# Zero rows written by ScalarE, four slots for the first token exponentials, and another order of SyncE's transfers in an attention and soft-mixture block

## The chip, the core and the metric

The kernel runs on one core of a Trainium2 chip. The metric is the device time of one execution in microseconds. Three runs of the kernel before took 2685.64, 2686.21 and 2699.97 us, median 2686.21 us. TensorE multiplies matrices, VectorE reduces and combines, ScalarE evaluates functions and copies, GpSimd does side work, and SyncE only waits on semaphores and issues transfers. Each engine runs its own list of instructions in order; semaphores tie the lists together.

## The reference

The input x is 4 sequences of 2048 tokens with 256 features. The output is the sum of x and two branches of its layer norm:

```
x  = L0_attn_x;  xn = layernorm(x)
q, k, v = xn @ wq.T, xn @ wk.T, xn @ wv.T        # 16 heads of 16, 4 groups of keys and values
att = softmax(causal(q k / 4));  attention = (att v) @ wo.T
y  = layernorm(xn) * g + b;  se = layernorm(slot_embeds) * slot_g + slot_b
logits[n, e, s] = y[n] . se[e, s]                # 2048 tokens by 16*64 = 1024 slots, per sequence
dispatch = softmax(logits over the tokens); combine = softmax(logits over the 1024 slots)
slots = dispatch.T @ y;  eout[e] = (gelu(slots Wg + bg) * (slots Wu + bu)) Wd + bd
out = x + attention + combine @ eout
```

## The kernel before

There are five parts, one after the other: `project` (the projections), `attend`, `dispatch`, `experts`, `combine`. `attend` and `dispatch` share one block, so that an engine goes from the one into the other without a barrier. The diff touches the start of `attend` and the first half of `dispatch`.

**attend.** The 16 pairs of a sequence and a group of keys ("bg") each take 40 steps; a step s is one block of 128 keys against one chunk of 512 queries, for 4 heads. TensorE fills a ring of 7 PSUM banks with row-maximum products ("x", read by VectorE) and with score products ("s", read by ScalarE's exponentials, line 857, which write `pr`, a buffer of 4 steps by 4 heads by 512). The "x" work runs 22 steps ahead (`LEAD`), so the first 22 steps (-22 to -1, the lead) hold only "x" and, in steps -17 to -2, the early logits "l": 16 half tiles of the first 8 token tiles of `dispatch`. ScalarE copies each out of the ring (L844) into `pr`, which is still free, four half tiles to a buffer, and issues its transfer to DRAM (L847). At step 0 ScalarE waits until all 16 have landed, as the exponentials then write `pr`.

Queries and keys stand in groups of 64 rows of which the upper 32 are mostly zero. For group 0 GpSimd writes the zeros in `project`; for groups 1 to 3 SyncE issues 12 transfers (L737) from a zero tile, at the start of `attend`. Then its loop issues the row maxima (L749, as each comes out of VectorE), the loads of groups 1, 2 and 3 at steps -6, 6 and 46 (L533 to L542), and the context stores (L755).

**dispatch.** Phases: L0, L1, P(0,0), P(0,1), L2, P(1,0), P(1,1), L3, P(2,0), P(2,1), P(3,0), P(3,1). In a phase L of a sequence b, TensorE makes the logits of 16 token tiles (8 in L0), 12 matmuls each (L1364), into two pairs of PSUM banks. ScalarE copies each to SBUF (L1224); VectorE takes the row maximum (L1282) and the running column maximum (L1290). ScalarE then makes the token exponentials (L1197) of 1024 slots, n counting the 64 tiles, into `e1`, and SyncE stores each to DRAM (L1123). `e1` has 2 slots, so exponential n waits until store n-2 has landed. L0 and L1 hold 32 exponentials for 24 tiles. In the last 6 tiles of L1, L2, L3, VectorE also subtracts the column maximum from a half tile of the sequence before (L1253), and ScalarE exponentiates it (`exp_tile`, L1169), behind its copy and token exponential.

In a phase P(b, half) TensorE multiplies 16 tiles of these exponentials with rows y (L1381). The rows come in pairs of tiles m: SyncE loads a pair (L1093) into one of 4 places as soon as the multiplication has released it (`d_free`), and ScalarE scales it (L1179). In P(b,0) the first six tiles were exponentiated ahead; ScalarE's list there starts with the scaling of the fifth pair and only then has the exponential of tile 6. SyncE's list for a phase L has, at every fourth tile (t % 4 == 2), the load of the next 512 columns of y transposed (L1083), which waits until TensorE has finished tile t+1; in the last two tiles the loads of the fifth and sixth pair of y rows for the coming P phase; and the stores of exponentials.

## Time and profile before

| quantity | value |
|---|---|
| median of three runs | 2686.21 us (2685.64 to 2699.97) |
| the profiled execution | 2682.58 us, its span 2680.9 us |
| TensorE, VectorE, ScalarE, GpSimd busy | 2562.2, 2037.7, 1696.6, 432.2 us |
| start of `attend` to step 0 | about 154 to 213 us |
| phases L0 and L1 | 1767.2 to 1863.3 us |
| phases P(0,0) to L2 to P(1,0) | from 1852.9, 1.8 us per tile in P |
| L3 and what follows in `dispatch` | to about 2197 us |

### The profile page before, as it was taken

The numbers are of one execution on the slowest core, as the hardware profiler recorded it, in microseconds if no ns is written. First come the engines' busy times: TensorE is split into PE (matmuls) and PEld (weight loads), VectorE is DVE, ScalarE is ACT, GpSimd is POOL, SyncE is SP. The second block draws the span as 40 slices with busy tenths as digits, with TensorE's granted clock in tenths as the row PEclk, the third lists the DMA queues.
The fourth block names the chain that finished last, engine by engine and source line by source line (L and its number), as shares of the span: only waits on it lengthen the run. The fifth ranks groups of instructions, "written<-read, shape, count | busy, mean of one in ns | idle before, by whom it ended". The sixth has DMA issues, their size and how long they took to land. (4 is left out here: it accounts for less than half of the span.)

```text
span 2680.9 us, 47835 instructions
## 1 busy us (share of the span) xinstructions
PE 2562.2 (96%) x16291; PEld 1526.7 (57%) x16291; DVE 2037.7 (76%) x4879; ACT 1696.6 (63%) x3506; POOL 432.2 (16%) x677
## 2 busy tenths in 40 slices
PE   7988999999999999999999999988989999999999
PEld 4553444444444444444444444356877888889999
DVE  8877989989988989999999998946465523356665
ACT  5526777777777778777777777876656652122221
POOL 6711111111111111111111111323020100100000
PEclk9988999999999999999999999999999999999999
DMA  8995243303303303312321001045333364445554
GB/s 267 321 227 79 37 52 45 44 7 45 45 6 45 45 12 41 45 22 30 45 33 18 8 8 70 30 157 181 122 134 144 104 200 142 156 163 192 192 191 149
DMA packets 184110, 258.21 MB, mean 96 GB/s; under 512 B 57780, under 2 KB 134200, under 8 KB 182360
## 3 DMA queue, kind: packets, MB, share of 16 engines
q1 hardware_dynamic: 166040, 236.64, 35.0%
q10 hardware_dynamic: 17856, 18.88, 2.4%
q8 instruction: 114, 1.87, 0.3%
q14 instruction: 100, 0.82, 0.1%
HBM read 160.40 MB, written 89.16 MB: 93 GB/s over the span
## 5 line engine op out<-in xcount | busy, mean ns | idle before, releaser
L857 ACT ACTIVATE att_pr<-att_ring 128x512 f32<-128x512 f32 (+3 forms) x2560 | 1174.2, 548 | 333.1 <-PE att_ring L956 314.5
L923 DVE TENSOR_REDUCE att_mx<-att_ring 128x1 f32<-128x512 f32 x1536 | 967.9, 680 | 85.9 <-PE att_ring L969 83.5
L969 PE MATMUL att_ring<-att_ks,w_queries 48*128 48x512 f32 (+3 forms) x1920 | 647.0, 422 | 18.4 <-ACT att_pr L857 8.5
L956 PE MATMUL att_ring<-w_queries,att_ks 64*128 64x512 f32 (+3 forms) x1920 | 575.8, 406 | 6.3 <-DVE att_mx L929 2.3
L956 PEld LDWEIGHTS att_ring<-w_queries,att_ks 64*128 64x128 f32 x1920 | 300.7, 186 | 403.1 <-DVE att_mx L923 145.1
L929 DVE CUSTOM_DVE_ANT_0 att_junk<-att_ring,w_causal 128x256 bf16<-128x256 f32 (+3 forms) x1024 | 466.1, 486 | 60.4 <-PE att_ring L969 34.2
L1009 PE MATMUL att_acc<-att_pr,att_v 128*17 128x512 f32 (+3 forms) x3840 | 453.6, 544 | 2.7 <-ACT att_cT L868 1.5
L969 PEld LDWEIGHTS att_ring<-att_ks,w_queries 48*128 48x128 f32 x1920 | 307.0, 185 | 143.8 <-ACT att_pr L857 104.7
L803 POOL TENSOR_SCALAR_AFFINE_SELECT att_pr<-att_pr 128x512 f32<-128x512 f32 x256 | 163.0, 637 | 1042.5 <-ACT att_pr L857 1042.5
L969 PE MATMUL att_ring<-g_ks,w_queries 48*128 48x512 f32 (+3 forms) x640 | 208.3, 435 | 22.6 <-ACT att_pr L857 12.9
L1631 ACT CAST com_e1h<-com_tp 128x1024 fp32r<-128x1024 f32 x64 | 64.7, 1016 | 238.1 <-PE com_tp L1691 238.1
L956 PE MATMUL att_ring<-w_queries,g_ks 64*128 64x512 f32 (+3 forms) x640 | 197.3, 409 | 2.1 <-DVE att_mx L929 0.8
L1707 PE MATMUL com_mp<-pre_parts,com_e1h 128*128 x1024 | 186.7, 283 | 3.7 <-DVE com_e1l L1656 3.7
L956 PEld LDWEIGHTS att_ring<-w_queries,g_ks 64*128 64x128 f32 x640 | 103.3, 188 | 135.3 <-DVE att_mx L923 49.3
L1707 PEld LDWEIGHTS com_mp<-pre_parts,com_e1h 128*128 128x128 f32 x1024 | 158.9, 191 | 4.3 <-issue 4.3
L1009 PE MATMUL att_acc<-att_pr,g_v 128*17 128x512 f32 (+3 forms) x1280 | 152.0, 547 | 0.0
L1707 PE MATMUL com_mp<-pre_parts,com_e1l 128*128 x512 | 144.7, 283 | 0.0
L1009 PEld LDWEIGHTS att_acc<-att_pr,att_v 128*17 128x17 f32 x3840 | 78.0, 117 | 112.9 <-ACT att_pr L857 72.3
L969 PEld LDWEIGHTS att_ring<-g_ks,w_queries 48*128 48x128 f32 x640 | 99.4, 192 | 67.1 <-ACT att_pr L857 39.4
L1364 PE MATMUL dis_ps<-w_seTh,w_yTh 128*128 128x512 f32 x224 | 93.5, 417 | 24.7 <-ACT dis_lg L1224 14.8
L1381 PE MATMUL dis_ps<-dis_y,pre_parts 128*128 128x257 f32 x512 | 112.6, 380 | 4.2 <-ACT pre_parts L1169 4.2
L1381 PE MATMUL dis_ps<-dis_y,dis_lg 128*128 128x257 f32 x512 | 112.3, 380 | 1.8 <-ACT dis_lg L1169 1.8
(181 smaller groups left out, 3243.0 us busy)
## 6 DMA issues: line engine op xcount, KB each, us to landing
slot_exps<-dis_e SPq DMA_DIRECT2D x64, 512.0 KB, 2.8
com_e<-slot_exps SPq DMA_DIRECT2D x64, 512.0 KB, 3.6
w_queries<-q_parts SPq DMA_DIRECT2D x96, 256.0 KB, 12.0
q_parts<-w_queries SPq DMA_DIRECT2D x32, 512.0 KB, 5.0
dis_y<-in_L_attn_x_dram SPq DMA_DIRECT2D x64, 256.0 KB, 2.8
att_ks<-k_parts SPq DMA_DIRECT2D x72, 128.0 KB, 12.8
y_cols<-proj_yT SPq DMA_DIRECT2D x16, 512.0 KB, 5.3
w_yTl<-y_cols SPq DMA_DIRECT2D x16, 512.0 KB, 4.2
```

The costliest lines, as they stand in the source:

```text
L803: nc.gpsimd.affine_select(out=blk, in_=blk, compare_op=ALU.is_ge, fill=0.0, base=0, pattern=[[0, GS], [1, P]], channel_multiplier=-1).then ...
L857: nc.scalar.activation(pr[:, s % NPR, h, off:CH], spot(("s", s, h)), ACT.Exp, scale=float(HD) ** -0.5).then_inc(exp_done, 1)
L923: nc.vector.tensor_reduce(dst, spot(e), AX.X, ALU.max).then_inc(mb_used, 1)
L929: nc.vector.tensor_tensor_reduce(junk[:, h % 2, 0:wd], spot(e), w["causal"][:, CH - wd:CH], 1.0, LOW, ALU.add, ALU.max, dst).then_inc(mb_u ...
L956: nc.tensor.matmul(spot(e), ks[g][r, kb * P:(kb + 1) * P], qs[g][r, c, hf * CH + off:(hf + 1) * CH], start=True, stop=True).then_inc(sT_re ...
L969: nc.tensor.matmul(spot(e), qs[g][r, c, q0:q0 + P], ks[g][r, j * CH:j * CH + wd], start=True, stop=True).then_inc(mb_ready, 1)
L1009: last = nc.tensor.matmul(acc[VW * h:VW * h + HD + 1, off:CH], v[bg % NKV][:, kb // TPC, :, kb % TPC], pr[:, n % NPR, h, off:CH], start=(n ...
L1364: last = nc.tensor.matmul(ps[:, i % 2, 2 * (t % 2) + h, :], lhs[:, n % RING, k, (t % TPC) * P:(t % TPC + 1) * P], w[rhs][:, k, h * 512:(h ...
L1381: last = nc.tensor.matmul(ps[:, i % 2, q, 0:D + 1], lgs[b % 2][:, t, (hf * HB + q) * P:(hf * HB + q + 1) * P], y[:, m % NY, t % 2, 0:D + 1 ...
L1631: nc.scalar.copy(e1h[:, q].rearrange("p s n -> p (s n)"), tp[:, q, 0:2, :].rearrange("p a n -> p (a n)")).then_inc(e1h_kept, 1)
L1707: last = nc.tensor.matmul(mp[:, q, 0:D], lhs[:, q, s, :], rhs[:, b, s, :], start=(s == 0 and rhs is eoh and lhs is e1h), stop=(s == SB - 1 ...
```

## The change

1. SyncE's 12 zero transfers and the zero tile go. ScalarE writes the zeros by copies of a zero column, 32 partitions by 2048 elements each, 18 in all: 6 (group 1) before its first step, and one behind each of the first 12 early-logit copies (groups 2 and 3).
2. The last four early-logit transfers count on a semaphore of their own: step 0 waits for the first 12, step 3 for the last four.
3. The loads of groups 1 and 2 move from steps -6 and 6 to -2 and 10; the rows of ones of groups 1 to 3 count on the semaphore of the loads.
4. `e1` gets 4 slots for exponentials 0 to 31 (2 afterwards, when slots 2 and 3 hold the slot vectors, `sl` and `slT`); exponential 2 waits also for all context stores.
5. In `dispatch` SyncE issues a phase's stores of exponentials ahead of the load of y transposed, which moves from t % 4 == 2 to t % 4 == 3, and the fifth and sixth pair of y rows come behind all stores of the phase.

```diff
-    FIRST_LOADS = {-6: 1, 6: 2, 46: 3}
+    FIRST_LOADS = {-2: 1, 10: 2, 46: 3}
+    L_LATE = NL - GS
+    ZP = (QW + S) // S
...
-            for g in range(1, NKV):
-                for rg in range(NRG):
-                    r = slice(RG * rg + 32, RG * (rg + 1))
-                    for dst, n in ((queries[r, g * QW:(g + 1) * QW], QW), (ks[g][r, :], S)):
-                        sp.dma_start(dst.bitcast(F32).rearrange("p (k n) -> p k n", n=D),
-                                     w["zero"][r, :].bitcast(F32).unsqueeze(1)
-                                     .to_broadcast([32, n // D, D])).then_inc(zeroed[g], 16)
...
+            def zero_rows(k):
+
+                g, rg, n = 1 + k // (NRG * ZP), k // ZP % NRG, k % ZP
+                r = slice(RG * rg + 32, RG * (rg + 1))
+                rows = ks[g][r, :] if n == ZP - 1 else queries[r, g * QW + n * S:g * QW + (n + 1) * S]
+                nc.scalar.copy(rows, w["causal"][r, 0:1].to_broadcast([32, S])).then_inc(zeroed[g], 1)
+
+            for k in range(NRG * ZP):
+                zero_rows(k)
...
                         nc.scalar.copy(half_tile(e[1]), spot(e)).then_inc(l_kept, 1)
+                        if e[1] < (NKV - 2) * NRG * ZP:
+                            zero_rows(NRG * ZP + e[1])
...
-                                      half_tile(e[1])).then_inc(l_out, 16)
+                                      half_tile(e[1])).then_inc(l_out if e[1] < L_LATE else l_late, 16)
                 if s == 0:
-                    act.wait_ge(l_out, 16 * NL)
+                    act.wait_ge(l_out, 16 * L_LATE)
+                if s == NPR - 1:
+                    act.wait_ge(l_late, 16 * (NL - L_LATE))
...
-        e1 = a.sb("e1", [P, 2, NS])
+        e1 = a.sb("e1", [P, 4, NS])
...
+        WIDE = 2 * TPB
+        place = lambda n: n % 4 if n < WIDE else n % 2
+        stores_before = lambda n: n // 4 if n < WIDE else (WIDE // 4) + (n - WIDE) // 2
...
-                        if t % TPC == TPC - 2:
+                        store_exps(exps_by(b, t) if b < 2 else b * TPB + t + 1)
+                        if t % TPC == TPC - 1:
                             load_yT(b * CPB + t // TPC + RING)
-                        if b and t >= TPB - FIRST_Y:
-                            load_y(2 * (b - 1) * PAIRS + t - (TPB - FIRST_Y) + NY)
-                        store_exps(exps_by(b, t) if b < 2 else b * TPB + t + 1)
...
                     if b:
                         store_exps(b * TPB + TPB)
+                        for n in range(FIRST_Y):
+                            load_y(2 * (b - 1) * PAIRS + n + NY)
...
+                n = b * TPB + t
+                if n == 2:
+                    context_stored(act)
+                if stores_before(n):
+                    act.wait_ge(e_out[place(n)], 16 * stores_before(n))
```

ScalarE at the start of `attend`, kernel before (`att_pr` takes the early-logit half tiles):

```order
L844 COPY att_pr<-att_ring 128x512
L847 DMA first_logits<-att_pr 128x512
L844 COPY att_pr<-att_ring 128x512
L847 DMA first_logits<-att_pr 128x512
L844 COPY att_pr<-att_ring 128x512
```

and after, at the same place (`w_queries` and `att_ks` get their zero rows):

```order
L839 CAST w_queries<-w_causal 32x2048 x2
L839 CAST att_ks<-w_causal 32x2048
L839 CAST w_queries<-w_causal 32x2048 x2
L839 CAST att_ks<-w_causal 32x2048
L847 COPY att_pr<-att_ring 128x512
L839 CAST w_queries<-w_causal 32x2048
L852 DMA first_logits<-att_pr 128x512
L847 COPY att_pr<-att_ring 128x512
L839 CAST w_queries<-w_causal 32x2048
L852 DMA first_logits<-att_pr 128x512
```

Six pieces stand ahead of the first copy now, and one piece between each copy and its transfer.

SyncE from the last stores of L1 into P(0,0), before (`slot_exps` are the exponentials' stores, `dis_y` the pairs of y rows, `w_yTl` y transposed):

```order
L1123 DMA slot_exps<-dis_e 128x1024 x5
L1083 DMA w_yTl<-y_cols 128x1024
L1093 DMA dis_y<-in_L_attn_x_dram 128x2x256
L1123 DMA slot_exps<-dis_e 128x1024
L1093 DMA dis_y<-in_L_attn_x_dram 128x2x256
L1123 DMA slot_exps<-dis_e 128x1024 x2
L1125 DMA slot_sums<-dis_zr 128x16
L1093 DMA dis_y<-in_L_attn_x_dram 128x2x256 x10
```

and after:

```order
L1135 DMA slot_exps<-dis_e 128x1024 x4
L1095 DMA w_yTl<-y_cols 128x1024
L1135 DMA slot_exps<-dis_e 128x1024
L1137 DMA slot_sums<-dis_zr 128x16
L1105 DMA dis_y<-in_L_attn_x_dram 128x2x256 x12
```

The two pairs of y rows that were issued among the last stores now stand behind the last store and the sums. At the end of L2 one more thing stands ahead of them:

```order
L1135 DMA slot_exps<-dis_e 128x1024 x4
L1137 DMA slot_sums<-dis_zr 128x16
L1095 DMA w_yTl<-y_cols 128x1024
L1105 DMA dis_y<-in_L_attn_x_dram 128x2x256 x12
L1112 DMA slots<-dis_e 128x256 x4
```

There the load of y transposed comes between the last store and the y rows.

## Rows read from the trace of the kernel before

**Rows 1.** The page, part 1: busy us (share) and instructions.
```profile
PE 2562.2 (96%) x16291; PEld 1526.7 (57%) x16291; DVE 2037.7 (76%) x4879; ACT 1696.6 (63%) x3506; POOL 432.2 (16%) x677
```
**Rows 2.** Busy time by stretch, with granted clock, DMA share and GB/s.
```profile
160.00:204.00 44.00, 43.42 (x175) 25.39 (x174) 42.07 (x119) 9.39 (x16) 5.93 (x11) 0.92 0.99 211
213.80:225.40 11.60, 11.60 (x58) 5.38 (x58) 9.63 (x23) 7.47 (x19) 2.97 (x6) 0.50 0.00 0
...
1825.00:1830.00 5.00, 0.38 (x1) 0.39 (x2) 0.41 (x1) 5.00 (x10) 1.74 (x1) 0.63 0.26 105
```
**Rows 3.** ScalarE's timeline from the early logits to step 3.
```profile
166.47 0.59 ACT L844 COPY att_pr<-att_ring 128x512 f32<-128x512 f32 x1 [17.01 <-PE att_ring L980]
...
192.38 0.33 ACTq L847 DMA_DIRECT2D first_logits<-att_pr  x1
...
200.55 0.59 ACT L844 COPY att_pr<-att_ring 128x512 f32<-128x512 f32 x1 [1.67 <-PE att_ring L980]
...
213.11 2.23 ACT L857 ACTIVATE att_pr<-att_ring 128x512 f32<-128x512 f32 x5 [11.97 <-DMA first_logits<-att_pr]
...
220.36 0.38 ACT L857 ACTIVATE att_pr<-att_ring 128x256 f32<-128x256 f32 x1 [1.88 <-PE att_ring L956]
```
**Rows 4.** The early-logit transfer of 192.38 alone: issue to landing.
```profile
DMA to landing us min/median/max: 14.7/14.7/14.7
```
**Rows 5.** SyncE's timeline: the first transfer of the load of group 1.
```profile
188.05 0.40 SPq L533 DMA_DIRECT2D w_queries<-q_parts  x1
```
**Rows 6.** The form next to a zero piece: the page, part 5.
```profile
L1631 ACT CAST com_e1h<-com_tp 128x1024 fp32r<-128x1024 f32 x64 | 64.7, 1016 | 238.1 <-PE com_tp L1691 238.1
```
**Rows 7.** Waits of ScalarE, then of TensorE, from 1735 to 1850: total, times, longest.
```profile
ACT dis_e L1197 <- DMA slot_exps<-dis_e: 16.2, 9, 3.0
...
PE dis_ps L1364 <- ACT dis_lg L1224: 11.0, 6, 6.0
```
**Rows 8.** TensorE's timeline in L0 and L1.
```profile
1767.55 0.39 PE L1364 MATMUL dis_ps<-w_seTl,w_yTh 128*128 128x512 f32 x1
1767.78 0.40 PE L1364 MATMUL dis_ps<-w_seTh,w_yTl 128*128 128x512 f32 x1
...
1829.62 0.80 PE L1364 MATMUL dis_ps<-w_seTh,w_yTh 128*128 128x512 f32 x1 [5.95 <-ACT dis_lg L1224]
```
**Rows 9.** ScalarE's timeline from L0 to the start of P(0,0).
```profile
1770.31 1.02 ACT L1224 COPY pre_parts<-dis_ps 128x1024 f32<-128x1024 f32 x1 [3.15 <-PE dis_ps L1364]
1771.22 1.16 ACT L1197 ACTIVATE dis_e<-pre_parts,w_nr 128x1024 f32<-128x1024 f32 x1
...
1824.64 4.03 ACT L1179 ACTIVATE dis_y<-dis_y,w_yb,w_ys 128x256 f32<-128x256 f32 x8
...
1834.30 1.01 ACT L1224 COPY dis_lg<-dis_ps 128x1024 f32<-128x1024 f32 x1 [1.55 <-PE dis_ps L1364]
...
1848.82 0.99 ACT L1224 COPY dis_lg<-dis_ps 128x1024 f32<-128x1024 f32 x1
...
1853.37 0.99 ACT L1224 COPY dis_lg<-dis_ps 128x1024 f32<-128x1024 f32 x1
...
1864.45 1.08 ACT L1179 ACTIVATE dis_y<-dis_y,w_yb,w_ys 128x256 f32<-128x256 f32 x2
```
**Rows 10.** TensorE's timeline, tiles 6 to 13 of P(1,0).
```profile
1981.24 14.11 PE L1381 MATMUL dis_ps<-dis_y,dis_lg 128*128 128x257 f32 x64 [0.80 <-ACT dis_lg L1169]
```
**Rows 11.** SyncE's timeline at the end of L1 and of L2.
```profile
1864.95 0.43 SPq L1125 DMA_DIRECT2D slot_sums<-dis_zr  x1
...
1979.87 0.43 SPq L1125 DMA_DIRECT2D slot_sums<-dis_zr  x1
```
**Rows 12.** The load of y rows issued at 1980.47 alone: issue to landing.
```profile
DMA to landing us min/median/max: 3.2/3.2/3.2
```
**Rows 13.** VectorE's subtraction L1253 in L2, beside GpSimd's work and without it.
```profile
1955.79 2.83 DVE L1253 TENSOR_TENSOR dis_lg<-dis_lg,w_cm 128x512 f32<-128x512 f32 x1
...
1962.49 0.68 DVE L1253 TENSOR_TENSOR dis_lg<-dis_lg,w_cm 128x512 f32<-128x512 f32 x1
```

More of the change, by code:

```diff
@@ L347, in _ @@
                 nc.gpsimd.memset(w["ones"][:].bitcast(F32), 1.0).then_inc(zeroed, 1)
-                nc.gpsimd.memset(w["zero"][:].bitcast(F32), 0.0).then_inc(zeroed, 1)
-                pool.wait_ge(zeroed, 5)
+                pool.wait_ge(zeroed, 4)
                 tri = w["causal"][:, CH - P:CH]
@@ L681, in attend @@
         c_out = [sem(f"c_out{c}") for c in range(CPB)]
-        ones_set = [g0["ones_set"]] + [sem(f"ones_set{g}") for g in range(1, NKV)]
+        ones_set = g0["ones_set"]
+        ONES = lambda g: 16 * 2 * NRG if g else 0
         nm_max, cols_high, cols_split = sem("nm_max"), sem("cols_high"), sem("cols_split")
         acc_zeroed, v_ones = sem("acc_zeroed"), sem("v_ones")
-        l_split, l_kept, l_out, l_in = (sem(n) for n in ("l_split", "l_kept", "l_out", "l_in"))
+        l_split, l_kept, l_out, l_late, l_in = (sem(n) for n in ("l_split", "l_kept", "l_out", "l_late", "l_in"))
         nr, cm, nr_ready, cm_done = (first_logits[n] for n in ("nr", "cm", "nr_ready", "cm_done"))
@@ L722, in load @@
             def load(b, g):
-                for _ in load_group(sp, scr, b, g, qs[g], ks[g], v[g], loaded[g], zeroed[g] and (zeroed[g], 16 * 2 * NRG)):
+                for _ in load_group(sp, scr, b, g, qs[g], ks[g], v[g], loaded[g], zeroed[g] and (zeroed[g], NRG * ZP)):
                     pass
@@ L727, in load_first @@
                 load(0, g)
-                for _ in load_ones(sp, w, ks[g], ones_set[g]):
+                for _ in load_ones(sp, w, ks[g], loaded[g]):
                     pass
@@ L950, in _ @@
                         if h == 0 and n % NU in first:
-                            if bg < NKV and c == 0:
-                                pe.wait_ge(ones_set[g], 16 * 2 * NRG)
+                            if bg == 0 and c == 0:
+                                pe.wait_ge(ones_set, 16 * 2 * NRG)
                             pe.wait_ge(m_rows[c], 16 * NRG * (bg + 1))
@@ L1046, in dispatch @@
         y = a.sb("y", [P, NY, 2, D + 2])
[L1047 to L1049 removed]
         zr = a.sb("zr", [P, 2, TPB])
         rz = a.sb("rz", [P, SB])
[L1052 to L1053 removed]
+        lgs = [pre["lg"], a.sb("lg", [P, TPB, NS])]
+        e1 = a.sb("e1", [P, 4, NS])
+        nr, cm, nr_ready, cm_done = (first_logits[n] for n in ("nr", "cm", "nr_ready", "cm_done"))
+        sl = e1[:, 2].rearrange("p (q d) -> p q d", q=HB)
+        slT = e1[:, 3].rearrange("p (q e k j) -> p q e k j", q=HB, e=2, k=DK)
         ps = a.ps("ps", [P, 2, 4, 512])
@@ L1057, in dispatch @@
         y_in = [sem(f"y_in{q}") for q in range(NY)]
-        e_out = [sem(f"e_out{q}") for q in range(2)]
+        e_out = [sem(f"e_out{q}") for q in range(4)]
         z_out = [sem(f"z_out{q}") for q in range(2)]
@@ L1122, in store_exps @@
                     sp.wait_ge(e1_ready, n + 1)
-                    sp.dma_start(scr["e1"][b, t], e1[:, t % 2]).then_inc(e_out[t % 2], 16)
+                    sp.dma_start(scr["e1"][b, t], e1[:, place(n)]).then_inc(e_out[place(n)], 16)
                     if t == TPB - 1:
@@ L1156, in _ @@
             context_stored(sp)
+            for q in range(4):
+                sp.wait_ge(e_out[q], 16 * (stores_before(B * TPB) if q < 2 else WIDE // 4))
             for q in range(2):
-                sp.wait_ge(e_out[q], 16 * B * TPB // 2)
                 sp.wait_ge(z_out[q], 16 * B // 2)
@@ L1773, in block_kernel @@
             queries = b.sb("queries", [P, NKV * QW], F32R)[:]
-            w["causal"], w["zero"] = b.sb("causal", [P, CH]), b.sb("zero", [P, D], F32R)
+            w["causal"] = b.sb("causal", [P, CH])
             w["wqT"], w["wkvT"] = b.sb("wqT", [P, DK, D]), b.sb("wkvT", [P, DK, P])
```

29 lines of the change are left out of this document (13 added, 16 removed).

## The prediction

> **What bounds the kernel now.** I read the page first: TensorE is busy for 96% of the span, VectorE 76%, ScalarE 63% [rows 1]. So a change can win only where TensorE stands still or runs at its lower clock, or where it is made to. The stretches around the edits show two such places. The first is step 0 of `attend`: from 160 to 204 TensorE and VectorE are busy nearly throughout (43.4 and 42.1 of 44 us), and from 213.8 to 225.4 TensorE is fully busy but at a granted clock of 0.50, 1.2 GHz [rows 2]. Between them ScalarE waits 11.97 us, from 201.1 to 213.11, for the early-logit transfers to land [rows 3]; the ring is full of scores it should have read, and TensorE idles about 9.7 us. The second is L0 and L1: ScalarE waits 16.2 us in 9 waits for stores of exponentials, and TensorE waits for its copies, 11.0 us in the group that shows the most, the longest 6.0 [rows 7]. In the P phases TensorE runs without a gap: 64 matmuls, 8 tiles, in 14.11 us, 1.76 us a tile [rows 10]. Whatever delays it there is lost for good.
>
> **Edit 1, the zero rows.** SyncE's 12 transfers go. They were over before 188, when the load of group 1 starts [rows 5], and no wait in that stretch is on them, since TensorE and VectorE are the full engines there. Their going is worth nothing. ScalarE gets 18 pieces of 2048 elements. The trace has no such copy. From the 512-wide copy (0.59) [rows 3] and the 1024-wide cast (1.016) [rows 6] the slope is 0.426 us per 512, so 2048 take 1.016 + 2 x 0.426 = 1.87 us, the low bound; twice the 1.16 us of the 1024-wide exponential that reads SBUF [rows 9] is 2.32, the high one. I take 1.87, being nearest in kind. The Trainium skill, "ScalarE: Activation LUTs", section "Table sets: the hidden batching unit", gives 186 ns plus 0.833 ns per element for an instruction with immediate scale and bias, 1.89 us for 2048 elements as an estimate, and no run here shows it yet; by it the sum would be the same.
>
> The first six take 11.2 us from the start of `attend` at about 154.4 and end at 165.7, before the first copy at 166.47, ahead of which ScalarE idles 17.01 us: hidden. The next 12 stand between copies that come every (200.55 - 166.47)/15 = 2.27 us [rows 3]. Copy and piece take 0.59 + 1.87 = 2.46, so ScalarE falls behind 0.19 us each, 2.3 in all. TensorE needs a bank again seven fills later, a bit more than a step, so a copy may be late by about 2.27 - 0.59 = 1.7 us. Cost on the path: 0.6, taken 0.5. At 2.32 a piece it is 12 x 0.64 - 1.7 = 6.0 us.
>
> **Edits 2 and 3, the wait at step 0.** The twelfth transfer was issued at 192.38 and landed 14.7 us later, at 207.1 [rows 3, 4]. It is slow because the load of group 1 runs from 188.05 [rows 5], and that stays: in SyncE's list nothing waits between the row maxima of step -8 and step -2, so the new number moves no transfer. With the copies late by a little I take 207.6. Step 0 starts there instead of at 213.11: -5.5 us. The last four land by 213.1; step 3 first needs their places at 220.36 - 5.5 = 214.9 [rows 3], so their wait costs nothing, with 1.8 us to spare. TensorE's idle falls from 9.7 to some 4 us, and the slow stretch of 11.6 us behind it shrinks. At full clock VectorE's 9.63 busy us would set its length [rows 2], so at most 2.0 us are to be had; I take 1.0. Start of `attend` in all: -5.5 - 1.0 + 0.5 = -6.0, bounds -8.5 and +0.5. The later load of group 2 and the ones have some 50 steps of slack and cost nothing.
>
> **Edit 4, four slots.** Matmuls of a logit tile follow each other at 0.233 us, 12 to a tile: 2.80 us [rows 8]. From the copy of the first tile of L0 (1770.31) to that of the eleventh of L1 (1834.30) are 18 tiles and 64.0 us [rows 9]; TensorE's own pace is 18 x 2.80 = 50.4. ScalarE's work there is 18 copies at 0.91 (1770.31 to 1771.22), 26 exponentials at about 1.15 and 4.03 of y rows [rows 9]: 16.4 + 29.9 + 4.0 = 50.3 us. They fit, if it never waits for a store, and four slots give a store over three exponentials' time and the copies between, some 5 us. The y rows come in one piece at tile 7 of L1: 0.9 + 2.3 + 4.0 = 7.2 against two tiles of room, 5.6, so 1.6 late. That leaves 64.0 - 50.4 - 1.6 = 12.0 us; a half-speed stretch after this stop takes 0.5 back. Gain 11.5, bounds 13.6 (nothing late) and 4 (only the longest wait goes, part of it). The six last tiles of L1 don't get faster: there copy, maximum, column maximum, subtraction and `exp_tile` form one chain between ScalarE and VectorE of 1853.37 - 1848.82 = 4.55 us a tile, whatever the stores do. The new wait of exponential 2 for the context stores ends near 1771, and it comes after 1773: nothing.
>
> **Edit 5, the order of SyncE's transfers.** The stores no longer stand behind a wait for TensorE; that is in the 11.5. But the fifth and sixth pair of y rows, issued before the last store until now, come behind it and the sums. In L1 the sums are issued at 1864.95 and take 0.43 [rows 11], so the pair goes out at 1865.4 and lands 3.2 later [rows 12], at 1868.6. ScalarE scales it at 1864.45 today [rows 9], as the first thing in P(0,0), and tile 6's exponential is behind it. So TensorE, through with tile 5, stands 4.1 us longer. In L3 the same, 4.1. In L2 the load of y transposed, 512 KB, goes out between: the sums at 1979.87 + 0.43, then some 1.1 more than in L1, 5.2 us; TensorE starts tile 6 at 1981.24 after 0.80 idle [rows 10]. Together 13.4 us, on the path, since TensorE never catches up in P. Each idle of near 5 us will also lower the clock: after the 5.95 us before 1829.62 [rows 8] the stretch 1825 to 1830 had a granted 0.63 [rows 2] and the matmuls behind it were slow. I take 1.5 us each, 4.5 (between 0 and 2.5 each). Cost 17.9, bounds 10 (landing at 2.5, no clock loss) and 22.
>
> The load of y transposed comes up to a tile later; the columns have 8 tiles of slack. It also moves GpSimd's splitting. In L2 the subtraction takes 2.83 us beside GpSimd's and 0.68 without [rows 13], in the ScalarE-VectorE chain. Two of the meetings in L1 and L2 fall behind the phase now: -1, bounds -3 and +2. The Trainium skill, "GPSIMD Engine Reference", section "Specifications", says that GpSimd shares its SBUF interfaces with VectorE, with contention for VectorE instructions of two SBUF inputs; the subtraction is one, and the trace agrees (2.83 against 0.68). By that rule only where the meetings fall matters, and each may cost as much as this one.
>
> **Sum.** -6.0 - 11.5 + 17.9 - 1.0 = -0.6 us on the profiled execution's 2682.58 (span 2680.9), that is 2682.0. That execution stands 3.6 below the median of 2686.21, so 2685.6 in terms of the runs.
>
> **Rivals.** *Faster: the y rows are not on the path.* If ScalarE's list hid the late pair, or the data came before its turn, -18.5 would be left: 2668. For it: SyncE has little else to do there. Against it: ScalarE has the scaling ahead of tile 6's exponential, and TensorE waits 0.80 us at just this place already [rows 10].
> *Slower: late y rows at full price.* Place: tile 6 of P(0,0), P(1,0), P(2,0). Each stop costs 5 us and more of landing and 2.5 of clock, 22 in all, while the gain of L0 and L1 is 9: -5 - 9 + 22 = +8, 2694. It decides as soon as the three stops together exceed the two gains, 17 to 18 us. For it: after 5.95 us idle the clock did fall.
> *Slower: zero pieces near 2.32 us.* The lead loses 6.0, the start of `attend` comes out at -0.5, and the sum is +5: 2691. For it: the SBUF-reading exponential is slower than the copies; against: it has an accumulator and a bias operand.
> *Four slots change little.* If the ScalarE-VectorE chain held the earlier tiles too, the gain were 4 instead of 11.5: +7, 2693. Against it: before tile 10 there is no subtraction in the chain.
>
> **Chances.** My case 0.55 (its own range 2679 to 2691), y rows hidden 0.17, y rows at full price 0.12, dear pieces 0.09, slots of little use 0.07. The range of 8 in 10 is 2671 to 2696: with the bounds of all terms it takes in most of the rivals. A measurement of this kernel tells a change from none at about 0.5%, 13.4 us. Faster than that needs the hidden y rows and little else against: 0.11. Slower needs two of the slow rivals together: 0.06. Within: 0.83.
>
> **What would show it.** In the profile after: ScalarE's pieces at 1.87 us; its wait before step 0 ending near 207 to 208 and none to speak of at step 3; no wait for stores in L0 and L1, 52 us instead of 64.0 from the first copy of L0 to the eleventh of L1; the chain of 4.55 unchanged; a wait of ScalarE of about 4 us for y rows at the start of P(0,0), P(1,0), P(2,0), with a gap of about 5 us in TensorE behind tile 5, and a low clock after it. If that gap is missing, the time is near 2668. If the two gains are missing, it is above 2696.

## The result, and the profile after

The changed kernel took 2700.06 us (median of 20 runs, 2690.79 to 2705.93), the kernel before, beside it on the same chip, 2688.36 (20 runs, 2680.35 to 2699.97). The ratio is 1.0039, 95% interval 1.0027 to 1.0050: slower by about 10.5 us, where -0.6 was predicted. The time lies outside the predicted range (2671 to 2696). It does so narrowly on the prediction's own base too: 2686.21 times 1.0039 is 2696.7. Of all runs of both kernels and of the experiments two took 4790.17 and 6806.88 us; every ratio leaves them out.

ScalarE has 33.7 busy us more, its 18 pieces; VectorE and GpSimd hardly moved. TensorE has 13.2 busy us more in a span 15.5 us longer [rows 1]. That is more busy time for the same 16291 instructions, and the granted clock below shows where it comes from.

```profile
span 2696.4 us, 47844 instructions
...
PE 2575.4 (96%) x16291; PEld 1535.2 (57%) x16291; DVE 2038.7 (76%) x4879; ACT 1730.3 (64%) x3524; POOL 433.9 (16%) x676
```

TensorE's timeline divides the rest of the kernel at the first matmul of each phase. The table gives the length of each stretch in us, in the profiled executions of the two kernels and of five of the experiments below. A column is read downward; its sum is the time from the start of L0 to the start of the expert stage.

| stretch | before | after | y rows back | only y rows late | slots only | y rows ahead of the last store | start edits only |
|---|---|---|---|---|---|---|---|
| L0 to P(0,0) | 85.71 | 78.73 | 78.87 | 89.36 | 78.79 | 79.15 | 85.28 |
| P(0,0) to L2 | 59.12 | 64.34 | 56.94 | 65.79 | 60.18 | 60.89 | 60.00 |
| L2 to P(1,0) | 56.61 | 54.81 | 54.67 | 54.35 | 56.54 | 54.55 | 56.26 |
| P(1,0) to L3 | 58.45 | 68.07 | 59.26 | 67.21 | 58.48 | 61.46 | 58.95 |
| L3 to P(2,0) | 51.10 | 53.04 | 52.65 | 51.05 | 51.38 | 52.84 | 51.07 |
| P(2,0) to experts | 120.70 | 128.47 | 120.69 | 128.92 | 120.71 | 121.45 | 121.84 |

After against before: -7.0, +5.2, -1.8, +9.6, +1.9 and +7.8, together +15.8. The three stretches that begin with a P phase lose 22.6; L0 and L1 gain 7.0. The whole attention gives 3.2 (1612.76 to 1609.56 from its first matmul to L0), and the stage ahead of it ended 3.7 later in this execution (158.18 against 154.45), which no edit explains: in the profiles of this study it ended anywhere from 153.9 to 162.2.

**The stops in the P phases.** TensorE's timeline of the kernel after at tile 6 of P(0,0), P(1,0) and P(2,0). In brackets stands the idle time ahead of a row.

```profile
1862.26 18.10 PE L1401 MATMUL dis_ps<-dis_y,pre_parts 128*128 128x257 f32 x70 [4.84 <-ACT pre_parts L1182]
...
1985.15 11.16 PE L1401 MATMUL dis_ps<-dis_y,dis_lg 128*128 128x257 f32 x38 [5.51 <-ACT dis_lg L1182]
...
2104.17 16.15 PE L1401 MATMUL dis_ps<-dis_y,pre_parts 128*128 128x257 f32 x60 [5.52 <-ACT pre_parts L1182]
```

ScalarE at the first of them, and SyncE just before it. ScalarE is done with the last exponential at 1856.2, waits 4.30 us for the y rows, and only then computes tile 6.

```profile
1856.03 0.19 ACT L1213 ACTIVATION_READ_ACCUMULATOR dis_e<-dis_lg,w_nr 128x1 f32 x1
1860.51 1.09 ACT L1192 ACTIVATE dis_y<-dis_y,w_yb,w_ys 128x256 f32<-128x256 f32 x2 [4.30 <-DMA dis_y<-in_L_attn_x_dram]
1861.51 1.13 ACT L1182 ACTIVATE pre_parts<-pre_parts 128x512 f32<-128x512 f32 x2
```
```profile
1856.24 0.33 SPq L1135 DMA_DIRECT2D slot_exps<-dis_e  x1
1856.61 0.43 SPq L1137 DMA_DIRECT2D slot_sums<-dis_zr  x1
1857.09 40.59 SPq L1105 DMA_DIRECT2D dis_y<-in_L_attn_x_dram  x12
```

The pair is issued 0.48 behind the sums and used 3.4 later: the predicted 0.43 [rows 11] and 3.2 [rows 12]. What follows each stop was not predicted in its size. Busy time and granted clock by stretch, behind the first stop, behind the stop of 1.95 us that P(1,0) has ahead of its long one, and behind the second and the third long stop (columns: stretch, length, TensorE busy, granted clock, DMA share, GB/s):

```profile
1862.30:1867.70 5.40, 5.40 (x13) 0.50 0.01 3
1870.00:1880.00 10.00, 10.00 (x48) 1.00 0.23 75
1976.90:1979.60 2.70, 2.70 (x7) 0.51 0.49 195
1985.20:1990.50 5.30, 5.30 (x13) 0.50 0.00 0
1994.00:2004.00 10.00, 10.00 (x48) 1.00 0.29 75
2104.20:2110.00 5.80, 5.80 (x14) 0.50 0.00 1
```

**L0 and L1.** The waits of the kernel after from 1735 to 1850 (total, times, longest). The waits for stores (16.2 us in nine [rows 7]) are gone, and TensorE's largest for its copies fell from 11.0 to 7.7 us. In their place ScalarE waits for VectorE's subtraction.

```profile
ACT pre_parts L1182 <- DVE pre_parts L1271: 11.8, 5, 3.5
...
PE dis_ps L1384 <- ACT dis_lg L1242: 7.7, 3, 2.8
```

**The start of `attend`.** ScalarE's timeline of the kernel after from the twelfth transfer to step 0, which answers to [rows 3], and the landing of that transfer alone [rows 4].

```profile
199.24 1.90 ACT L839 CAST att_ks<-w_causal 32x2048 fp32r<-32x2048 f32 x1
199.25 0.34 ACTq L852 DMA_DIRECT2D first_logits<-att_pr  x1
...
215.21 1.08 ACT L864 ACTIVATE att_pr<-att_ring 128x512 f32<-128x512 f32 x2 [8.21 <-DMA first_logits<-att_pr]
```
```profile
DMA to landing us min/median/max: 15.9/15.9/15.9
```

A piece takes 1.90 us where 1.87 was taken. The Trainium skill, "ScalarE: Activation LUTs", section "What ACT_TABLE_LOAD costs" (the prediction names the section behind it), has 186 ns plus 0.833 ns per element for an ACTIVATE with immediate scale and bias, an estimate of 1.89 us for 2048 elements; the trace agrees. Step 0 begins 57.0 us after the start of `attend` (before: 58.7), so 1.6 of the predicted 5.5 came.

### The profile page after: what moved, and what is told of

Same layout as the page of the kernel before. It is cut to its first block and busy times, and to the rows that moved or that the text cites. A ratio compares the mean times of both kernels' runs of the same rounds, so it can differ in the third digit from the quotient of the medians.

```text
span 2696.4 us, 47844 instructions
## 1 busy us (share of the span) xinstructions
PE 2575.4 (96%) x16291; PEld 1535.2 (57%) x16291; DVE 2038.7 (76%) x4879; ACT 1730.3 (64%) x3524; POOL 433.9 (16%) x676
## 3 DMA queue, kind: packets, MB, share of 16 engines
q8 instruction: 114, 1.87, 0.3%
## 5 line engine op out<-in xcount | busy, mean ns | idle before, releaser
L976 PE MATMUL att_ring<-g_ks,w_queries 48*128 48x512 f32 (+3 forms) x640 | 210.3, 436 | 17.1 <-ACT att_pr L864 7.6
L976 PEld LDWEIGHTS att_ring<-g_ks,w_queries 48*128 48x128 f32 x640 | 100.4, 192 | 64.0 <-ACT att_pr L864 33.7
L1401 PE MATMUL dis_ps<-dis_y,pre_parts 128*128 128x257 f32 x512 | 118.3, 394 | 11.5 <-ACT pre_parts L1182 11.5
L1192 ACT ACTIVATE dis_y<-dis_y,w_yb,w_ys 128x256 f32<-128x256 f32 x128 | 69.5, 597 | 79.9 <-DMA dis_y<-in_L_attn_x_dram 79.9
## 6 DMA issues: line engine op xcount, KB each, us to landing
att_ks<-k_parts SPq DMA_DIRECT2D x72, 128.0 KB, 12.8
```

Source lines behind the costliest of these rows:

```text
L976: nc.tensor.matmul(spot(e), qs[g][r, c, q0:q0 + P], ks[g][r, j * CH:j * CH + wd], start=True, stop=True).then_inc(mb_ready, 1)
L1192: nc.scalar.activation(rows, rows, ACT.Identity, scale=w["ys"][:, n, t + u:t + u + 1], bias=w["yb"][:, n, t + u:t + u + 1]).then_inc(y_rea ...
L1401: last = nc.tensor.matmul(ps[:, i % 2, q, 0:D + 1], lgs[b % 2][:, t, (hf * HB + q) * P:(hf * HB + q + 1) * P], y[:, m % NY, t % 2, 0:D + 1 ...
```

## The experiments

Theory A after the result: the y rows behind the last store cost over 20 us, more than all the gains. Rival B: the zero pieces and the new start of `attend` cost what is missing. Rival C: four slots, or the stores put first, bring nothing. Ratios are to the kernel before that ran beside them, with 95% intervals.

### Y rows back (label y_back)

The changed kernel with one edit:

```
                     for t in range(first_tile(b), TPB):
+                        if b and t >= TPB - FIRST_Y:
+                            load_y(2 * (b - 1) * PAIRS + t - (TPB - FIRST_Y) + NY)
                         store_exps(exps_by(b, t) if b < 2 else b * TPB + t + 1)
...
                         store_exps(b * TPB + TPB)
-                        for n in range(FIRST_Y):
-                            load_y(2 * (b - 1) * PAIRS + n + NY)
```

> The changed kernel with one thing undone: the fifth and sixth pair of y rows are issued in tiles 14 and 15 of L1, L2, L3 again, ahead of that tile's stores. Theory A (late y rows are what the change pays with): the gaps of 4.8, 5.5 and 5.5 us at tile 6 of P(0,0), P(1,0), P(2,0) fall below 1 us, with the slow clock behind them; the stretches P(0,*), P(1,*), P(2,*) to P(3,*) go from 64.3, 68.1 and 124.6 us back to about 59, 58.5 and 117; the kernel is some 20 us faster than the changed one and 8 to 10 us faster than before (about 2678). Rival B (the moved loads of y transposed and GpSimd's work at new times cost it): at most 5 us faster than the changed one.

Measured: 2676.75 us (2671.36 to 2679.48), ratio 0.9948 (0.9933 to 0.9962). It was run a second time beside a version of it that follows below:

> The changed kernel with its y rows back in tiles 14 and 15, a second time, so that it runs beside the version with the gate on one chip: 2675 to 2679, as at first (2676.8).

Measured: 2676.00 us (2675.43 to 2680.60), ratio 0.9952 (0.9938 to 0.9966). This version beats both kernels, by some 13 us and 23 us. Its stretches in the table differ from those of the kernel after by 7.4, 8.8 and 7.8 us at the P phases and by at most 0.4 elsewhere. SyncE issues the first pair 3.66 us after the phase's start and the second at 7.13, between the stores, and TensorE has 0.52 us idle where it had 4.84. (In the second profile it has 1.11 and 0.66 there, and P(0,0) to L2 takes 58.43 instead of 56.94.)

```profile
1847.64 0.39 SPq L1105 DMA_DIRECT2D dis_y<-in_L_attn_x_dram  x1
1848.07 0.47 SPq L1135 DMA_DIRECT2D slot_exps<-dis_e  x1
```
```profile
1855.07 20.18 PE L1401 MATMUL dis_ps<-dis_y,pre_parts 128*128 128x257 f32 x92 [0.52 <-ACT pre_parts L1182]
```

### Only the y rows late (label y_late_only)

The kernel before with the same lines the other way round:

```
-                        if b and t >= TPB - FIRST_Y:
-                            load_y(2 * (b - 1) * PAIRS + t - (TPB - FIRST_Y) + NY)
...
                         store_exps(b * TPB + TPB)
+                        for n in range(FIRST_Y):
+                            load_y(2 * (b - 1) * PAIRS + n + NY)
```

> The kernel before with this one edit alone: fifth and sixth pair of y rows behind all stores of the phase. Theory A: tile 6 of P(0,0), P(1,0), P(2,0) waits 4 to 5 us for ScalarE's scaling, then 3 to 7 us at half the clock; 18 to 23 us slower than before (about 2708). Rival B: within 5 us of before. Rival C (the stops are only this dear because the phases L end sooner in the changed kernel): 5 to 10 us slower.

Measured: 2709.90 us (2703.06 to 2716.99), ratio 1.0067 (1.0048 to 1.0086). The P stretches grow by 6.7, 8.8 and 8.2. Two of the stops:

```profile
1882.12 8.21 PE L1381 MATMUL dis_ps<-dis_y,pre_parts 128*128 128x257 f32 x29 [4.33 <-ACT pre_parts L1169]
...
2002.38 7.99 PE L1381 MATMUL dis_ps<-dis_y,dis_lg 128*128 128x257 f32 x22 [5.62 <-ACT dis_lg L1169]
```

So this one move costs 18 to 24 us with the other edits or without them. A holds both ways; B and C are not needed for the sign, and the C of this run (5 to 10 us) is out.

### Four slots alone (label slots_only)

The kernel before with the slots, and with the ones rows counted on the loads' semaphores:

```
-        e1 = a.sb("e1", [P, 2, NS])
+        e1 = a.sb("e1", [P, 4, NS])
+        sl = e1[:, 2].rearrange("p (q d) -> p q d", q=HB)
+        slT = e1[:, 3].rearrange("p (q e k j) -> p q e k j", q=HB, e=2, k=DK)
...
-                    act.wait_ge(e_out[t % 2], 16 * ((b * TPB + t) // 2))
+                if n == 2:
+                    context_stored(act)
+                if stores_before(n):
+                    act.wait_ge(e_out[place(n)], 16 * stores_before(n))
```

> The kernel before with four slots for the first 32 exponentials alone (the rows of ones of groups 1 to 3 count on the loads' semaphore, as in the changed kernel, to free semaphores); SyncE's order as before, so a store can still stand behind a load that waits for TensorE. If the slots alone make the gain: first to nineteenth copy (L0's first to L1's eleventh) in 53 us instead of 64, and the kernel 7 to 10 us faster than before. If SyncE's order is half of it: 57 to 60 us for these, and 3 to 6 us faster.

Measured: 2682.48 us (2674.46 to 2688.92), ratio 0.9965 (0.9951 to 0.9978), -9.4 us. The stretch L0 to P(0,0) has 78.79 us, as in the kernel after (78.73): the slots alone make all of the gain there. They make somewhat more, for in this profile L0 began at half clock, and its first copy came 5.5 us after the phase's start instead of 3.1:

```profile
1766.90:1772.20 5.30, 5.29 (x13) 0.50 0.59 160
```

From there the eleventh copy of L1 comes after 54.8 us (before 64.0), and behind it nothing is given back: 18.46 us to P(0,0), before 18.62. Without that loss of 2.4 us the slots gain 9.3. C falls, as far as the slots go.

### The start of `attend` alone (label attend_only)

The kernel before with edits 1 to 3, that is ScalarE's zero pieces, the first exponentials' own waits and the moved loads:

```
+                nc.scalar.copy(rows, w["causal"][r, 0:1].to_broadcast([32, S])).then_inc(zeroed[g], 1)
...
-    FIRST_LOADS = {-6: 1, 6: 2, 46: 3}
+    FIRST_LOADS = {-2: 1, 10: 2, 46: 3}
...
-                    act.wait_ge(l_out, 16 * NL)
+                    act.wait_ge(l_out, 16 * L_LATE)
+                if s == NPR - 1:
+                    act.wait_ge(l_late, 16 * (NL - L_LATE))
```

> The kernel before with all edits of the start of attend and none in dispatch. From the profiles of before and after I expect the wait before step 0 to end 57 us after the start of attend instead of 58.7, less slow clock behind it, and 3 us gained in all (2685), which 5 rounds may not tell from nothing. A rival: the later starts cost as much as they give, the difference is zero or a loss of 1 to 2 us.

Measured: 2687.99 us (2681.03 to 2692.33), ratio 0.9990 (0.9982 to 0.9999), -2.7 us. B falls: these edits cost nothing. But they bring little; step 0 begins 58.7 us after the start of `attend`, as before.

```profile
212.60 2.23 ACT L864 ACTIVATE att_pr<-att_ring 128x512 f32<-128x512 f32 x5 [8.45 <-DMA first_logits<-att_pr]
```

### The stores' order beside the slots (label slots_stores)

The kernel before with four slots and SyncE's stores ahead of the rest of each tile. The y pairs stay in tiles 14 and 15, but behind that tile's store, where the version with the y rows back has them ahead of it.

```
-                        if t % TPC == TPC - 2:
+                        store_exps(exps_by(b, t) if b < 2 else b * TPB + t + 1)
+                        if t % TPC == TPC - 1:
                             load_yT(b * CPB + t // TPC + RING)
                         if b and t >= TPB - FIRST_Y:
                             load_y(2 * (b - 1) * PAIRS + t - (TPB - FIRST_Y) + NY)
```

> The kernel before with four slots for the exponentials and the changed order of SyncE's stores and of the transposed y tiles, but with all y rows in tiles where they stood, and with none of the edits at the start of attend. Four slots alone gave 2682.5 and 78.8 us for the stretch from the first tile of L0 to the second phase of pair 0. If the order of the stores has no worth of its own, this version is within 1.5 us of 2682.5; if the stores first shorten the waits at the tails, it is 2 to 4 us below; if the transposed tiles now come late, above 2684 with a wait ahead of the transposed products.

Measured: 2688.47 us (2677.37 to 2693.63), ratio 0.9988 (0.9975 to 1.0002), so 6 us worse than the slots alone. The stores' order gains nothing in L0 and L1 (80.40 us against 78.79), and P(1,0) to L3 takes 63.74 where the slots alone have 58.48. There the first pair goes out at 1977.27, behind its tile's store, and the second at 1982.2, behind the last store, the sums and the load of y transposed:

```profile
1977.27 0.43 SPq L1099 DMA_DIRECT2D dis_y<-in_L_attn_x_dram  x1
1980.53 0.33 SPq L1129 DMA_DIRECT2D slot_exps<-dis_e  x1
...
1981.38 0.79 SPq L1089 DMA_DIRECT2D w_yTl<-y_cols  x1
1982.21 1.22 SPq L1099 DMA_DIRECT2D dis_y<-in_L_attn_x_dram  x2
```
```profile
1988.40 7.78 PE L1396 MATMUL dis_ps<-dis_y,dis_lg 128*128 128x257 f32 x27 [2.28 <-ACT dis_lg L1177]
```

With the y rows back, each pair ahead of its tile's store, the same stretch has 59.26: one place in a queue decides 4.5 us here.

### Y rows ahead of the last store alone (label y_before_last)

The kernel after, but the last store follows the y rows:

```
-                        store_exps(exps_by(b, t) if b < 2 else b * TPB + t + 1)
+                        store_exps(exps_by(b, t) if b < 2 else b * TPB + min(t + 1, TPB - 1))
...
-                        store_exps(b * TPB + TPB)
+                        store_exps(b * TPB + TPB - 1)
                         for n in range(FIRST_Y):
                             load_y(2 * (b - 1) * PAIRS + n + NY)
+                        store_exps(b * TPB + TPB)
```

> The changed kernel, but the fifth and sixth pair of y rows are issued behind the store of tile 14 and ahead of the store of the half's last tile. In the changed kernel SyncE stood at that store until 1856.2 and issued the first pair at 1857.1; here it can issue it at about 1853.4, 3.7 earlier. If the whole price is SyncE's wait for the last tile's exponentials, TensorE's stops of 4.8, 5.5 and 5.5 us shrink to 1 to 2 each, with them the half-speed stretches, and the time falls by 15 to 20 us, to 2680 to 2685. Rival (the rows are slow because ten more pairs and the stores go out beside them, whatever the order): stops over 3 us stay, and the time is 2688 to 2700.

Measured: 2684.08 us (2674.15 to 2688.05), ratio 0.9977 (0.9964 to 0.9990). The time is where the first theory has it, the stops are not quite: they shrink to 3.1, 2.9 and 1.4. The first pair goes out at 1858.08, 8.2 us after the phase's start, in the kernel after 10.6. TensorE's stops at tile 6, and the granted clock behind the first two:

```profile
1859.86 1.97 PE L1402 MATMUL dis_ps<-dis_y,pre_parts 128*128 128x257 f32 x8 [1.10 <-ACT pre_parts L1183]
1864.96 15.41 PE L1402 MATMUL dis_ps<-dis_y,pre_parts 128*128 128x257 f32 x70 [3.13 <-ACT pre_parts L1183]
...
1980.97 9.34 PE L1402 MATMUL dis_ps<-dis_y,dis_lg 128*128 128x257 f32 x42 [2.85 <-ACT dis_lg L1183]
...
2092.99 12.38 PE L1402 MATMUL dis_ps<-dis_y,pre_parts 128*128 128x257 f32 x56 [1.41 <-ACT pre_parts L1183]
```
```profile
1868.00:1872.00 4.00, 4.00 (x21) 1.00 0.22 66
1984.00:1988.00 4.00, 4.00 (x21) 1.00 0.24 66
```

### The load of group 1 held back (labels before_gate, y_back_gate, y_back_gate_2)

One wait more in SyncE's list, once in the kernel before and once in the version with the y rows back:

```
             def load_first(g):
+                if g == 1:
+                    sp.wait_ge(l_kept, NL)
                 load(0, g)
```

The wait ends when ScalarE has made its last copy of the early logits, not, as the expectations say, when all transfers have landed; only the last of them still runs beside the load.

> The kernel before, word for word, with one more wait: SyncE issues the load of group 1 only when all first transfers of the logits' tiles have landed. Theory (the twelfth transfer is slow because that load is issued beside it): the transfer's 14.7 us fall to 2 to 5, ScalarE's two waits for transfers there (16.2 us together) to below 6, and the time falls by 6 to 12 us, to 2678 to 2684. Rival (the fills of zero rows, which stand in SyncE's queue ahead of the load, are what holds the transfer up in this kernel): a wait over 10 us stays, and the time is within 2 us of before.

Measured: 2681.96 us (2680.11 to 2684.89), ratio 0.9969 (0.9957 to 0.9981). The load starts at 209.23, 48.9 us after the start of `attend` (before 33.6), ScalarE's wait ahead of step 0 is 5.19, and step 0 begins 54.1 us after the start of `attend`, 4.6 sooner. ScalarE's wait and the longest landings of the last six transfers:

```profile
214.40 2.23 ACT L859 ACTIVATE att_pr<-att_ring 128x512 f32<-128x512 f32 x5 [5.19 <-DMA first_logits<-att_pr]
```
```profile
DMA to landing us min/median/max: 2.0/2.0/5.1
```

The fills of zero rows were still there, so they are not what holds the twelfth transfer up. (They do slow the first ones: the first six land after 4.6 to 6.7 us here, after 2.0 to 2.7 in the kernel after, which has no fills.)

> The changed kernel with its fifth and sixth pair of y rows back in tiles 14 and 15, and with one more wait: SyncE issues the load of group 1 only when all first transfers of the logits' tiles have landed. Theory (the twelfth transfer is held up by the load that is issued beside it): ScalarE's wait of 8.2 us for it just ahead of step 0 shrinks to 0 to 2, TensorE's gap there (5.9 us) to about 1, and the time falls by 4 to 7 us against the version without the gate (2676.8), to 2670 to 2673. Rival (the transfer is late because ScalarE issues it late, 3.1 us of lag from the zero pieces, and it takes its time anyway): the wait stays over 5 us and the time within 2 us of 2676.8. A third outcome, the load of group 1 comes too late for its own steps: a new wait at the first steps of group 1, and over 2678.

Measured: 2678.34 us (2666.12 to 2681.94), ratio 0.9952 (0.9934 to 0.9970). The wait goes as the theory has it; the time does not follow.

> The same with the load of group 1 held back until the logits' first transfers have landed. In its profile the transfers took 2.0 us, step 0 came 8.5 us sooner after the start of the attention, but the medians of the two versions stood 1.6 us apart in the wrong direction, in runs of two different calls. If the gate's gain is real in every execution, this version is 5 to 9 us below the one without it, on the same chip; if something gives it back (the first steps at half speed, a project stage that ends later), the two are within 2 us.

Measured: 2677.47 us (2666.68 to 2683.68), ratio 0.9946 (0.9927 to 0.9966), beside 2676.00 without the gate. In the trace the wait for the transfers is gone; step 0 begins 49.1 us after the start of `attend` in both profiles (57.6 and 57.1 without the gate), and the attention ends 8.4 and 3.5 us sooner after its start.

```profile
205.01 1.17 ACT L866 ACTIVATE att_pr<-att_ring 128x512 f32<-128x512 f32 x2 [0.49 <-PE att_ring L965]
```

The half clock behind step 0 stays, although TensorE has no gap over 0.3 us ahead of it any more. TensorE in the first of these profiles:

```profile
204.40:209.50 5.10, 4.27 (x18) 1.00 0.79 158
209.60:219.70 10.10, 10.10 (x50) 0.50 1.02 112
```

The whole kernel is not faster for it. In the second profile L0 to P(0,0) takes 83.25 us instead of 77.4, with stops of 4.1 and 4.5; in the first it takes 77.0. Whether the gate leads to that, or two profiles happen to differ, is open. The gate pays in the kernel before; on top of the y rows' old place no gain could be measured.

### Zero pieces on GpSimd (labels attend_pool, y_back_gate_pool)

The zero pieces written by GpSimd, one for each step of the lead:

```
-                nc.scalar.copy(rows, w["causal"][r, 0:1].to_broadcast([32, S])).then_inc(zeroed[g], 1)
+                nc.gpsimd.memset(rows.bitcast(F32), 0.0).then_inc(zeroed[g], 1)
+                pool.wait_ge(zeroed[g], 1 + k % (NRG * ZP))
...
             for s in ALL_STEPS:
+                if s + LEAD < (NKV - 1) * NRG * ZP:
+                    before = [e for x in ALL_STEPS if x < s for e in m_events(x)]
+                    if before:
+                        pool.wait_ge(nm_ready, len(before))
+                    zero_rows(s + LEAD)
```

> The kernel before with the changed kernel's edits at the start of attend alone, but the zero pieces are written by GpSimd (one memset for each step of the lead) and not by ScalarE. If the pieces on ScalarE hold its logits' copies up by 3 us (the copy period was 2.54 us with them, 2.27 before), the twelfth copy comes 41.1 - 3.1 = 38 us after the start of attend again and the time falls 2 to 3 us below that of the version with ScalarE's pieces (2688.0). Rival (ScalarE had room, the wait on the transfer swallows the difference): within 1 us of 2688.0. Against it: GpSimd's writes hold up its split of the row maxima or VectorE's copies beside it, and the time is above 2689.

Measured: 2689.21 us (2684.52 to 2695.86), ratio 0.9997 (0.9984 to 1.0011): the case against it. Four pieces stand ahead of GpSimd's part of the row maxima, which TensorE waits for. GpSimd's timeline, then TensorE's:

```profile
165.76 3.65 POOL L797 MEMSET w_queries<- 32x2048 f32 x2
...
171.32 1.80 POOL L797 MEMSET w_queries<- 32x2048 f32 x1
173.18 0.20 POOL L830 CAST att_nml<-att_nm 128x16 fp32r<-128x16 f32 x1
```
```profile
173.83 0.37 PE L995 MATMUL att_ring<-w_ident,att_nml 128*32 128x128 f32 x1 [6.28 <-POOL att_nml L832]
```

> The changed kernel with its y rows back in tiles 14 and 15, the gate for the load of group 1, and the zero pieces on GpSimd. If both the lag of ScalarE (3 us) and the load beside the twelfth transfer (4 to 7 us) count, 2667 to 2671; if only the load counts, the same as the version with the gate alone; if GpSimd's writes disturb the start, 1 to 3 us above that version.

Measured: 2678.21 us (median of 6 runs, 2672.53 to 6806.88), ratio 0.9948 (0.9928 to 0.9968), no different from the version with ScalarE's pieces; its profile has the same stop, 6.37. What the lag of ScalarE alone costs thus stays unmeasured: this placement brought a stop of its own.

## Why the prediction was wrong

Four terms were off, all to the same side: by the stretches of the two profiles the y rows by 4.7 us (22.6 for 17.9), the slots by 4.5 (7.0 for 11.5), the start by 2.8 (3.2 for 6.0) and GpSimd's moved splitting by 1.1.

**Edit 5, the late y rows: the step that failed is its clock term.** Place, mechanism and wait were right. Against the version with the y rows back, TensorE's waits there grow by 4.3 (4.84 for 0.52), 4.9 (1.95 + 5.51 for 1.95 + 0.66) and 4.9 (1.11 + 5.52 for 1.10 + 0.67), 14.0 us together; the prediction had 13.4. But the three stretches grow by 7.4, 8.8 and 7.8, 24.0. The difference, 10.0 us, is work at half clock, where the prediction took 4.5, 1.5 a stop "(between 0 and 2.5 each)". (Against the second profile with the y rows back it is 22.5 of time, 12.8 of waits, 9.7 of clock.) It is seen directly: behind the long stops TensorE works 5.4, 5.4 and 5.9 us at 0.50, of which half is lost, and 2.7 us more behind the stop of 1.95 us in P(1,0). For the size the prediction went by one stop, the 5.95 us ahead of 1829.62 [rows 8], and the row that it quotes, 1825 to 1830 at 0.63 [rows 2], lies mostly inside that stop. The trace of the kernel before right behind it:

```profile
1829.60:1833.10 3.50, 3.48 (x8) 0.50 0.38 150
```

Matmuls follow each other there at 0.43 us instead of 0.23, about 1.6 us lost. So 1.5 was right for that stop and wrong as the size of others. Five stops of 5.5 to 6.1 us in L1 of these kernels are followed by 2.9 to 4.2 us of half clock; the long stops at tile 6, in the kernel after and in the one with only the y rows late, by 4.7 to 6.0 in five cases and in the sixth by 3.4, with 2.5 more ahead of the stop. What makes the difference is open. The other stop that the prediction shows, 9.7 us at step 0 with 11.6 us at 0.50 behind it [rows 2], should have widened the bounds. So the edit costs 24 instead of 17.9 in the profiles; between the versions' medians it is 23.3 (2700.06 - 2676.75), and 19.2 when made alone (2709.90 - 2690.66).

**Edit 4, four slots: 11.5 predicted, 7.0 in the profile after, 9.3 with the slots alone.** (The runs with the slots alone say 9.4, between 5.9 and 13.2.) From the first copy of L0 (1770.84) to that of the eleventh tile of L1 (1824.12) are now 53.3 us; "52 instead of 64.0" was predicted. The 10.7 gained there are partly given back in L1's last tiles: from that copy to P(0,0) it takes 22.35 us, before 18.62. Of these 3.7 us, 2.7 are the late start of the chain: VectorE's column maximum falls beside GpSimd's splitting, where it takes 3.42 us instead of 1.21, and the next copy waits for the subtraction behind it. That next copy comes 7.27 us after the eleventh tile's; in the kernel before it is 4.57, and 4.57 with the slots alone too, where SyncE's order is the old one. The other 1.0 is half clock in the last tile. Rows of VectorE, GpSimd and ScalarE of the kernel after:

```profile
1824.54 3.42 DVE L1310 TENSOR_TENSOR w_cm<-w_cm,dis_lg 128x1024 f32<-128x1024 f32 x1
...
1829.02 1.21 DVE L1310 TENSOR_TENSOR w_cm<-w_cm,dis_lg 128x1024 f32<-128x1024 f32 x1
```
```profile
1824.47 2.40 POOL L1331 TENSOR_TENSOR w_yTl<-w_yTl,w_yTh 128x1024 fp32r<-128x1024 f32 x1
```
```profile
1830.86 0.63 ACT L1182 ACTIVATE pre_parts<-pre_parts 128x512 f32<-128x512 f32 x1 [3.45 <-DVE pre_parts L1271]
```

The prediction had the effect, for the subtraction [rows 13], and held the last tiles fixed at 4.55 us each. Most are, once the chain runs (one in the kernel after and two in the one before take 5.39); what it missed is how late the chain now starts. Its count of 26 exponentials up to the eleventh copy is also off, there are 24; they fit all the more.

**Edits 2 and 3, the wait at step 0: 5.5 predicted, 1.6 in the profile after, nothing in that of the start edits alone.** Two things failed. Pieces and copies come every 2.53 us in place of 2.27, so the twelfth transfer is issued 41.1 us after the start of `attend` instead of 37.9; the prediction had 2.3 us of lag, and then took the transfer's landing as late only "by a little", 0.5. And the transfer, issued behind more of the load of group 1, took 15.9 us where 14.7 was assumed: it landed at 215.2, among the load's last parts (213.8 to 216.8). That it is this load, the kernels with the gate show: the twelfth transfer took 2.0 us in all of them. The Trainium skill, "DMA: Bandwidth & Descriptors", section "Issuing engines are not separate DMA queues", says that transfers started by different engines interleave on the same 16 DMA engines; the trace agrees, with a transfer of ScalarE's queue at 15.9 us beside SyncE's load and 2.0 without it. Behind step 0 the attention is 1.6 us shorter (1.0 was predicted), as the slow stretch is 0.68 over 10.2 us instead of 0.50 over 11.6 [rows 2]. That the stop is what lowers the clock there is not shown: with the gate the stop is gone and the half clock is not.

```profile
216.00:226.20 10.20, 9.97 (x58) 4.95 (x58) 8.46 (x22) 7.30 (x19) 2.96 (x6) 0.68 0.08 25
```

**Edit 1 and the late columns.** The pieces' price was right. For the moved load of y transposed -1 was predicted. L3 to P(2,0) takes 52.3 to 53.3 us in the eight profiles with the new order and 51.05 to 51.38 in the six without it. In the kernel after, GpSimd's splitting now falls on the column maximum just ahead of the chain, at 31.1 us into L3 (before 25.1), and the chain's first subtraction comes 38.7 us into L3 (before 36.8). It is the same meeting as in L1, and the prediction had looked for meetings with the subtraction only. L2 to P(1,0) scatters by 2.3 us among kernels that are alike there (56.61 before, 54.32 with the gate), so its 1.8 us less says nothing.

```profile
2064.80 3.18 DVE L1310 TENSOR_TENSOR w_cm<-w_cm,dis_lg 128x1024 f32<-128x1024 f32 x1
```

**The sum.** By the runs of single parts: start -2.7, slots -9.4, late y rows +24.5 (from 0.9948 to 1.0039 of 2688), together +12.4; measured +10.5 (7.3 to 13.4). The prediction missed by 11 us. Term by term the y rows' price was 6.6 too low, the start and the slots 5.4 too good (12.1 for 17.5), and the 1 for GpSimd's moved splitting did not come; these make 13, 2 more than the miss, within the interval. The rival "late y rows at full price" had it right: 22 us for three stops, and the point from which it decides, 17 to 18 us, was passed, with gains of 12. It rested on the same single stop as the smaller term, and with nothing to choose between the two it deserved more than 0.12.

## What to carry to other kernels

Where a queue of transfers is put in a new order, price each one that is moved behind a wait by who uses it next, before the gain is counted: here two pairs of loads moved behind the last stores turned -13 us into +10. On a TensorE that is otherwise full, 3 to 5 us of added stop cost 6 to 9 us, since work behind it ran at half clock. Read that from the matmuls right behind several stops of the trace, not from one and not from the clock of a stretch around it: the one stop taken here as the model lost 1.6 us, the new ones 2.7 to 2.9 each. And a wait that ends with a transfer was not cured here by waiting for fewer of them, while a large load of another queue ran beside it: look at what was issued in the same microseconds.

## What was not expected of the hardware

The clock's answer to a stop is uneven. In P(0,0), 4.84 us idle at one time brought 0.50 behind it, while 1.10 and 3.13 us with 1.97 us of matmuls between them left it at 1.00, though TensorE resumed tile 6 only 0.75 us sooner. In P(1,0) of the kernel with the changed stores' order, gaps of 1.95, 0.92 and 2.28 us one after the other were followed by 0.65 over 4 us:

```profile
1988.00:1992.00 4.00, 3.60 (x10) 0.65 0.08 28
```

Of the fourteen stops of 1.94 to 1.96 us that the P phases of all profiles hold, seven were followed by half clock within 1.3 us (one is in P(1,0) of the kernel after, at 1976.4) and seven were not (one is in P(1,0) of the version with the y rows back, at 1966.4). And in the version with the gate half clock came without a stop at all, for 10.1 us from 209.6. Each fall in a P phase takes one to three us of the span, so two profiles of one kernel can differ by that much.

A VectorE maximum of 128x1024 elements nearly tripled, 1.21 to 3.42 us, beside a GpSimd subtraction of the same size.
